# Half-precision row transposes by transposing DMAs in a cross-attention and expert kernel

## The chip, the cores and the metric

One core of a Trainium2 chip runs the kernel. The metric is device time in microseconds of one execution. The kernel before takes 740.51 us, the median of 3 runs (737.42 to 745.31).

## What is computed

The reference is one layer on 2048 tokens of width 512: a cross-attention with 32 heads of 16, then a feed-forward part with one shared expert and 16 routed ones, of which each token takes two. Cut to what matters:

```
x = x + xattn(layernorm(x), ctx, pos)          # 32 heads of 16, axial RoPE
h = layernorm(x)                               # the "xn2" of the kernel
shared = (silu(h @ s1.T) * (h @ s3.T)) @ s2.T  # inner width 352
scores = sigmoid(h @ gate_w.T); top 2 of scores + bias, gates = sel / sum(sel)
routed = sum over chosen e of gate * ((silu(h @ w1[e].T) * (h @ w3[e].T)) @ w2[e].T)
x = x + shared + routed
```

## The kernel before

All engines run programs written out by hand, joined by semaphores. Every operand of a large product is split into a high and a low half-precision part, and a product is three matmuls per chunk of 128 (high by high, high by low, low by high). A matmul needs its rows with the model width on the partitions, so each [128 tokens, 2 parts, 512] tile of `xn2` must be transposed in eight 128x128 blocks.

**Attention** is a pipeline over 16 batches of 128 tokens. At its end, ScalarE makes the high part of `xn2` (`xn2_high`) and POOL the low part (`xn2_low`). PE then transposes both (`xn2_transpose`, line 622), ScalarE copies the result from PSUM into `xn2T` (`xn2T_copy`, line 828), and PE multiplies it with the gate weights (`gate_logits`). The first gate and up of the feed-forward part waits for all logits. SP's queue stores `xn2_parts` to HBM as `xn2_dram` and `xn2T` as `xn2T_dram`, and loads `ctx`.

**Shared stage.** The 16 tiles of 128 tokens are sub-tiles n = 0 to 15, two to a pair j. The order on PE is written out: hidden transpose of n (line 699), gate and up of n + 1 (line 692, into `p_qk` and `p_sc`), down of n (line 712). The operand `xeT` of gate and up has two buffers and is loaded from `xn2T_dram`: the first two by SP, the other 14 by ScalarE (`load_rows`, line 944), which issues the load for n + 2 after the gate activation of n + 1. Beside it DVE works out the routing.

**Routed stage.** Tokens are sorted by expert into tiles of 256 slots (two sub-tiles); this input needs 19 tiles, so 38 sub-tiles. POOL gathers the rows of a sub-tile from `xn2_dram` into `xe` (`gather`, line 1472) and scatters the results into the output with addition (`add_rows`, line 1487). PE transposes the gathered rows (`rows_transpose`, line 678) between gate and up and down, and ScalarE copies them from PSUM into `xeT` (`xeT_copy`, line 912). ScalarE and DVE also split the next expert's weights into parts (lines 933 and 940, 1100 and 1096). SP loads an expert's weights (1408 KB for gate and up, 704 KB for down) only where the tile's expert is a new one.

## Time and profile before

| | |
|---|---|
| median of 3 runs | 740.51 us |
| profiled execution | 740.43 us, span 738.7 us |
| mean granted clock of PE | 0.976 |
| busy: PE, DVE, ACT, POOL | 92%, 71%, 54%, 50% of the span |
| attention | 0 to 373 us |
| shared stage | 373 to 476 us |
| routed stage | 476 us to the end |

The busy shares are of the profiled execution's span. PE, TensorE's matmuls, is busy nearly all the time in each stage, except in the first 45 us and at the end of attention (340 to 373 us), where it waits for other engines. A wait is read from the brackets behind a row of the timeline: how long the engine was idle before it, and what released it.

### The profile page before, as it was taken

Reading aid. Unit: us, or ns where it says so; the run is one execution under the profiler, and the core shown is the slowest. Engines: PE = TensorE matmul, PEld = TensorE weight load, DVE = VectorE, ACT = ScalarE, POOL = GpSimd, SP = SyncE. Lnnn points to the kernel's source line nnn. Section 1 sums busy time; section 2 is a strip of 40 time slices with the busy share of each in tenths; the row PEclk is TensorE's granted clock in tenths of the full one; section 3 lists DMA queues with packets and bytes.
Section 4 is the critical chain, followed back from the end, with each engine's and each line's share of the span. In section 5 each row is a group of like instructions: output and inputs, shape, how many; then the busy total and the mean of one; then the engine's idle time right before and its main releaser. Section 6 shows DMA issues by size and latency. Waiting matters only on the chain.

```text
span 738.7 us, 20567 instructions
## 1 busy us (share of the span) xinstructions
PE 681.3 (92%) x7616; PEld 436.3 (59%) x7616; DVE 525.3 (71%) x992; ACT 397.6 (54%) x666; POOL 366.1 (50%) x439
## 2 busy tenths in 40 slices
PE   3389999999999999998489998999999999999992
PEld 1156666666666666666245665666666666666661
DVE  5968888888888888876537772467676666767671
ACT  4255666665666666665521111366666656666661
POOL 5455556655556665542100001145776557777662
PEclk9789999999999999999979999999999999999997
DMA  9610111000011110000113256258568875555952
GB/s 300 222 48 9 37 38 39 34 21 35 21 35 35 35 35 28 28 29 31 59 57 100 72 182 225 73 145 250 97 192 239 254 199 94 98 94 78 278 121 31
DMA packets 37601, 73.88 MB, mean 100 GB/s; under 512 B 3920, under 2 KB 8048, under 8 KB 37552
## 3 DMA queue, kind: packets, MB, share of 16 engines
q1 hardware_dynamic: 26736, 48.81, 19.2%
q0 software_dynamic: 8800, 20.73, 14.9%
q10 hardware_dynamic: 2016, 3.67, 1.7%
q8 instruction: 33, 0.54, 0.3%
q14 instruction: 16, 0.13, 0.1%
HBM read 69.85 MB, written 22.81 MB: 125 GB/s over the span
## 4 chain that ended last, share of the span: by engine, by line
PE 83%; DVE 6%; DMA 4%; issue 3%; POOL 2%; ACT 1%; POOLq 0%; SPq 0%; DVEq 0%; ACTq 0%
PE p_sc L712 13%; PE p_qk L692 13%; PE p_sc L692 12%; PE p_v L486 8%; PE p_qk L486 7%; PE p_pv L586 5%; PE p_st L534 4%; PE p_pv L589 4%; PE p_sc L566 3%; PE p_sc L549 3%; PE p_pv L596 2%; PE p_tr L678 2%; PE p_v L699 2%; PE p_sc L569 2%; DMA xeT<-xn2T_dram 2%
## 5 line engine op out<-in xcount | busy, mean ns | idle before, releaser
L809 ACT ACTIVATE prob<-p_sc 128x512 f32<-128x512 f32 x128 | 71.4, 601 | 58.8 <-PE p_sc L569 58.8
L1073 DVE TENSOR_REDUCE negmax<-p_sc 128x4 f16<-128x512 f32 x128 | 82.7, 685 | 8.6 <-PE p_sc L549 8.0
L924 ACT CAST hiddenT<-p_v 128x384 f16<-128x384 f32 x54 | 25.9, 479 | 108.7 <-PE p_v L699 108.7
L712 PE MATMUL p_sc<-used_twice,hiddenT 128*128 128x512 f16 (+1 forms) x342 | 80.1, 379 | 0.0
L1192 DVE TENSOR_TENSOR hidden<-p_sc,act_g 128x352 f32<-128x352 f32 x55 | 28.8, 524 | 68.5 <-PE p_sc L692 47.0
L1467 POOL COPY from_at<-from_rows 128x1 uint32 (+1 forms) x40 | 33.0, 825 | 89.0 <-DVE from_rows L1309 85.8
L692 PE MATMUL p_sc<-used_twice,xeT 128*128 128x352 f16 x468 | 76.2, 313 | 0.0
L692 PE MATMUL p_qk<-used_twice,xeT 128*128 128x352 f16 x468 | 76.2, 312 | 0.0
L1487 POOL DMA_INDIRECT out<-prob,to_at x38 | 67.8, 1786 | 11.0 <-issue 10.1
L1100 DVE SCALAR_TENSOR_TENSOR used_twice<-w,used_twice 128x704 f16<-128x704 f32 x80 | 67.7, 887 | 2.5
L692 PEld LDWEIGHTS p_sc<-used_twice,xeT 128*128 128x128 f16 x468 | 45.8, 98 | 24.0
L486 PE MATMUL p_qk<-used_twice,xnT 128*128 128x512 f16 x192 | 51.7, 396 | 8.5 <-issue 8.5
L912 ACT COPY xeT<-p_tr 128x1024 f16<-128x1024 f16 x40 | 40.5, 1013 | 34.2 <-PE p_tr L678 33.8
L933 ACT ACTIVATE used_twice<-w 128x704 f16<-128x704 f32 x80 | 58.6, 783 | 0.0
L692 PEld LDWEIGHTS p_qk<-used_twice,xeT 128*128 128x128 f16 x468 | 45.7, 98 | 20.5
L1446 POOL TENSOR_TENSOR xn_parts<-xn,xn_parts 128x512 f16<-128x512 f32 x16 | 18.5, 1156 | 70.8 <-ACT xn_parts L836 70.8
L586 PE MATMUL p_pv<-prob,used_twice_too 128*32 128x128 f32 x1024 | 52.6, 277 | 0.5 <-DVE attn L1092 0.5
L1209 DVE TENSOR_SCALAR prob<-p_sc,gate_at 128x512 f32<-128x512 f32 x38 | 28.5, 751 | 33.4 <-PE p_sc L712 30.8
L589 PE MATMUL p_pv<-prob,sum_row 128*32 128x128 f32 x1024 | 51.5, 273 | 0.0
L712 PEld LDWEIGHTS p_sc<-used_twice,hiddenT 128*128 128x128 f16 (+1 forms) x342 | 31.8, 98 | 31.5
L486 PE MATMUL p_v<-used_twice,attnT 128*128 128x512 f16 x192 | 47.6, 380 | 2.0 <-POOL attnT L1442 2.0
L1472 POOL DMA_INDIRECT xe<-xn_dram,from_at x40 | 45.4, 1135 | 8.1 <-issue 3.6
(186 smaller groups left out, 1551.3 us busy)
## 6 DMA issues: line engine op xcount, KB each, us to landing
w<-e SPq DMA_DIRECT2D x20, 1408.0 KB
w<-e SPq DMA_DIRECT2D x20, 512.0 KB
out<-stream SPq DMA_DIRECT2D x17, 256.0 KB, 2.1
xn_dram<-xn_parts SPq DMA_DIRECT2D x16, 256.0 KB, 2.0
xn2T_dram<-xn2T SPq DMA_DIRECT2D x16, 256.0 KB, 2.0
w<-e SPq DMA_DIRECT2D x20, 192.0 KB
stream<-x SPq DMA_DIRECT2D x1, 3584.0 KB, 16.8
xeT<-xn2T_dram ACTq DMA_DIRECT2D x14, 256.0 KB, 2.7
```

What stands on the lines that cost most here:

```text
L486: mm = pe.matmul(to, rows[:, r_part, c, :], w[:, w_part, c, :], start=(c == 0 and r_part + w_part == 0), stop=(c == last and r_part == 1))
L586: pe.matmul(p_pv[2 * HD * n:2 * HD * (n + 1), block], vpad[:, par, head(c, n), :], prob[:, c % RING, n * P:(n + 1) * P], start=(c % 4 == 0 ...
L589: mm = pe.matmul(pv_sum[2 * HD * n:2 * HD * (n + 1), :], sum_row[:, c % 4, :], prob[:, c % RING, n * P:(n + 1) * P], start=False, stop=(c ...
L692: mm = pe.matmul(p_out, xeT[:, u, x_part, c, :], w[:, w_part, c, at:at + INNER], start=(c == 0 and x_part + w_part == 0), stop=(c == KC - ...
L712: mm = pe.matmul(p_y[u][:], hiddenT[0:k, h_part, c, :], w[0:k, w_part, c, :], start=(c == 0 and h_part + w_part == 0), stop=(c == len(ICH) ...
L809: act.activation(prob[:, c % RING, :], p_scored(c)[:], ACT.Exp, scale=SCALE).then_inc(exp_ready, 1)
L912: act.copy(xeT[:, u], p_xT).then_inc(sems.xeT_ready, 1)
L933: act.activation(split[par][0][:, 0, c], w13[:, par, c], ACT.Copy, scale=W_SCALE).then_inc(hi13, 1)
L1073: dve.tensor_reduce(negmax[:, c % 2, at:at + CH], p_scored(c)[:].rearrange("p (h t) -> p h t", t=P), AX_X, ALU.max, negate=True).then_inc( ...
L1100: dve.scalar_tensor_tensor(to[0][:, 1, c], w13[:, par, c], W_SCALE, to[0][:, 0, c], ALU.mult, ALU.subtract).then_inc(lo13, 1)
L1472: pool.indirect_dma_start(out=xe[:, u].rearrange("p a d -> p (a d)"), out_offset=None, in_=xn2_dram, in_offset=bass.IndirectOffsetOnAxis(a ...
L1487: pool.indirect_dma_start(out=out, out_offset=bass.IndirectOffsetOnAxis(ap=to_at[:, par, u:u + 1], axis=0), in_=ye[:, par, u], in_offset=N ...
```

## The change

In attention SP's queue transposes `xn2_parts` from SBUF straight into `xn2T` behind the store of the same rows; PE's transposes and ScalarE's copy are gone, and so is `xn2T_dram`. In the shared stage the loads of `xeT` become transposing DMAs from `xn2_dram`. In the routed stage ScalarE issues a transposing DMA from `xe` into `xeT`, in the place of its copy, once the gather has landed and the buffer is free (`rows_turn`); a copy of one column into `carrier_act` stands ahead of it and carries the waits. POOL's next gather into `xe` waits for that DMA to land where it waited for PE. ScalarE issues its first transposing DMA after those of SP have landed.

```diff
--- before.py
+++ after.py
@@ -65,8 +65,6 @@
     def __init__(self, sem):
         self.xT_loaded = [sem(f"xT_loaded{n}") for n in range(2)]
         self.xe_gathered = [sem(f"xe_gathered{n}") for n in range(2)]
-        self.xeT_done = sem("xeT_done")
-        self.xeT_ready = sem("xeT_ready")
         self.g_done = sem("g_done")
         self.u_done = sem("u_done")
         self.act_ready = sem("act_ready")
@@ -91,7 +89,6 @@
 
 
         xn2_dram = nc.dram_tensor("xn2_dram", [T, 2 * DIM], F16, kind="Internal").ap()
-        xn2T_dram = nc.dram_tensor("xn2T_dram", [T, 2 * DIM], F16, kind="Internal").ap()
 
 
         stream = sb("stream", [P, B, DIM])
@@ -113,7 +110,7 @@
         ones16 = sb("ones16", [P, P], F16)
 
 
-        carrier_dve, carrier_pool = sb("carrier_dve", [P, 1]), sb("carrier_pool", [P, 2 * SUB + 1])
+        carrier_dve, carrier_act, carrier_pool = sb("carrier_dve", [P, 1]), sb("carrier_act", [P, SUB + 1]), sb("carrier_pool", [P, 2 * SUB + 1])
         minus_half = sb("minus_half", [P, 1])
         angle = sb("angle", [P, B, ROT])
         turns = sb("turns", [P, B, ROT])
@@ -257,9 +254,9 @@
 
         attnT_hi = sem("attnT_hi"); attnT_lo = sem("attnT_lo"); gate_parts = sem("gate_parts")
         wo_done = sem("wo_done"); ln2_step = sem("ln2_step"); rstd2_ready = sem("rstd2_ready")
-        xn2T_done = sem("xn2T_done"); xn2T_ready = sem("xn2T_ready")
+        xn2T_ready = sem("xn2T_ready")
         xn2_hi = sem("xn2_hi"); xn2_lo = sem("xn2_lo")
-        xn2_stored = sem("xn2_stored"); xn2T_stored = sem("xn2T_stored"); gate_done = sem("gate_done"); logits_kept = sem("logits_kept")
+        xn2_stored = sem("xn2_stored"); gate_done = sem("gate_done"); logits_kept = sem("logits_kept")
 
         gate_exp = sem("gate_exp"); route = sem("route"); masks_ready = sem("masks_ready")
         counted = sem("counted"); experts_known = sem("experts_known"); slots_known = sem("slots_known")
@@ -398,11 +395,8 @@
                 sp.wait_ge(xn2_stored, b * 16 + 16)
                 sp.dma_start(xn2_dram[bass.ds(b * P, P)], xn2_parts[:, par].rearrange("p a d -> p (a d)")).then_inc(xn2_stored, 16)
 
-            def store_xn2T(b, par):
-                sp.wait_ge(xn2T_ready, b + 1)
-                if later(b, 1):
-                    sp.wait_ge(xn2T_stored, b * 16)
-                sp.dma_start(xn2T_dram[bass.ds(b * P, P)], xn2T[:].rearrange("p a c t -> p (a c t)")).then_inc(xn2T_stored, 16)
+            def turn_xn2(b, par):
+                sp.dma_start_transpose(xn2T[:].rearrange("p a c t -> p (a c) t"), xn2_parts[:, par].rearrange("p a d -> p (a d)")).then_inc(xn2T_ready, 16)
 
             def load_ctx(b, half):
                 if later(b, 2):
@@ -413,11 +407,11 @@
             def step(b, on):
                 on(4, load_ctx)
                 on(-1, store_xn2)
-                on(-1, store_xn2T)
+                on(-1, turn_xn2)
                 if isinstance(b, int) and b == B - 1:
-                    sp.wait_ge(xn2T_stored, 2 * 16)
+                    sp.wait_ge(xn2_stored, 3 * 16)
                     for n in range(2):
-                        sp.dma_start(xeT[:, n].rearrange("p a c t -> p (a c t)"), xn2T_dram[n * P:(n + 1) * P]).then_inc(sems.xT_loaded[n], 16)
+                        sp.dma_start_transpose(xeT[:, n].rearrange("p a c t -> p (a c) t"), xn2_dram[n * P:(n + 1) * P]).then_inc(sems.xT_loaded[n], 16)
 
             load_ctx(2, 0)
             load_ctx(3, 1)
@@ -610,20 +604,13 @@
                 if c == KC - 1:
                     mm.then_inc(wo_done, 1)
 
-            def xn2_transpose(b, par):
-                pe.wait_ge(xn2_lo, b + 1)
+            def gate_logits(b, par):
+                pe.wait_ge(xn2T_ready, b * 16 + 16)
 
                 last_xn = B if isinstance(b, int) and b + 4 > B else b + 4
                 pe.wait_ge(xnT_lo, last_xn)
                 if later(b, 1):
                     pe.wait_ge(logits_kept, b)
-                for a in range(2):
-                    for c in range(KC):
-                        mm = pe.transpose(p_xT[:, a, c, :], xn2_parts[:, par, a, c * P:(c + 1) * P], ident16[:])
-                mm.then_inc(xn2T_done, 1)
-
-            def gate_logits(b, par):
-                pe.wait_ge(xn2T_ready, b + 1)
                 if not later(b, 1):
                     pe.wait_ge(gate_parts, 2)
                 for c in range(KC):
@@ -637,7 +624,6 @@
                 on(-3, spread_recip, 1)
                 on(-1, project_q, 0)
                 on(-2, scores, 2)
-                on(-4, xn2_transpose)
                 on(-1, project_q, 1)
                 on(-2, scores, 3)
                 on(-1, project_q, 2)
@@ -671,19 +657,10 @@
             pipeline(step, pe, 0, B + 3, 6, (B - 6) // 2, ahead=[xn_transpose])
 
 
-            def rows_transpose(n, u, j):
-                pe.wait_ge(sems.xe_gathered[u], (j - (SHARED - 1)) * 16)
-                for a in range(2):
-                    for c in range(KC):
-                        mm = pe.transpose(p_xT[:, a, c, :], xe[:, u, a, c * P:(c + 1) * P], ident16[:])
-                mm.then_inc(sems.xeT_done, 1)
-
             def gate_up(n, u, j, par, kind):
 
-                if kind == "shared":
-                    pe.wait_ge(sems.xT_loaded[u], j * 16 + 16)
-                else:
-                    pe.wait_ge(sems.xeT_ready, n - (B - 1))
+                pe.wait_ge(sems.xT_loaded[u], j * 16 + 16)
+                if kind == "routed":
                     pe.wait_ge(lo13, split_no(j) * KC)
                 w = split["shared" if kind == "shared" else par][0]
                 for p_out, at, done in ((p_g, 0, sems.g_done), (p_u, INNER, sems.u_done)):
@@ -743,8 +720,6 @@
                         gate_up(n + 1, 1, j, par, kinds[0])
                     elif kinds[1]:
                         gate_up(n + 1, 0, j + 1, 1 - par, kinds[1])
-                    if kinds[1] == "routed":
-                        rows_transpose(n + 2, u, j + 1)
                     down(n, u, j, par, kinds[0])
                     if kinds[0] == "shared":
                         if n == COUNTED:
@@ -820,19 +795,12 @@
                     act.wait_ge(wo_done, b)
                 act.copy(attnT[:, 0], attn_rows).then_inc(attnT_hi, 1)
 
-            def xn2T_copy(b, par):
-                act.wait_ge(xn2T_done, b + 1)
-                if later(b, 1):
-                    act.wait_ge(gate_done, b)
-                    act.wait_ge(xn2T_stored, b * 16)
-                act.copy(xn2T[:], p_xT).then_inc(xn2T_ready, 1)
-
             def xn2_high(b, par):
                 act.wait_ge(ln2_step, b * 5 + 5)
                 if later(b, 1):
                     act.wait_ge(xn2_stored, b * 16)
                 if later(b, 2):
-                    act.wait_ge(xn2T_done, b - 1)
+                    act.wait_ge(xn2T_ready, b * 16 - 16)
                 act.copy(xn2_parts[:, par, 0], xn2[:, par]).then_inc(xn2_hi, 1)
 
             def ctx_high(b, par):
@@ -870,7 +838,6 @@
             act.wait_ge(zeroed, 1)
 
             def step(b, on):
-                on(-5, xn2T_copy)
                 on(0, ctx_high)
                 on(-2, v_copy)
                 on(-3, exp, 0)
@@ -906,10 +873,11 @@
             act.wait_ge(logits_kept, B)
             act.activation(score[:], logits[:], ACT.Exp, scale=-1.0).then_inc(gate_exp, 1)
 
-            def xeT_copy(n, u):
-                act.wait_ge(sems.xeT_done, n - (B - 1))
+            def rows_turn(n, u, j):
+                act.wait_ge(sems.xe_gathered[u], (j - (SHARED - 1)) * 16)
                 act.wait_ge(sems.u_done, n - 1)
-                act.copy(xeT[:, u], p_xT).then_inc(sems.xeT_ready, 1)
+                act.copy(carrier_act[:, u:u + 1], minus_half[:])
+                act.dma_start_transpose(xeT[:, u].rearrange("p a c t -> p (a c) t"), xe[:, u].rearrange("p a d -> p (a d)")).then_inc(sems.xT_loaded[u], 16)
 
             def gate_act(n):
                 act.wait_ge(sems.g_done, n + 1)
@@ -941,9 +909,11 @@
 
             def load_rows(n, u):
                 act.wait_ge(sems.u_done, n - 1)
-                act.dma_start(xeT[:, u].rearrange("p a c t -> p (a c t)"), xn2T_dram[n * P:(n + 1) * P]).then_inc(sems.xT_loaded[u], 16)
-
-            act.wait_ge(xn2T_stored, B * 16)
+                act.dma_start_transpose(xeT[:, u].rearrange("p a c t -> p (a c) t"), xn2_dram[n * P:(n + 1) * P]).then_inc(sems.xT_loaded[u], 16)
+
+            act.wait_ge(xn2_stored, B * 16 + 16)
+            for n in range(2):
+                act.wait_ge(sems.xT_loaded[n], 16)
             gate_act(0)
 
             def pair(j, par, kinds):
@@ -960,7 +930,7 @@
                 if kinds[1] == "shared":
                     load_rows(n + 2, 0)
                 elif kinds[1]:
-                    xeT_copy(n + 2, 0)
+                    rows_turn(n + 2, 0, j + 1)
                 hT_high(n + 1)
                 if split_next:
                     w2_high(j + 1, 1 - par, 0)
@@ -972,9 +942,15 @@
                 if kinds[1] == "shared":
                     load_rows(n + 3, 1)
                 elif kinds[1]:
-                    xeT_copy(n + 3, 1)
-
-            pairs(pair, act)
+                    rows_turn(n + 3, 1, j + 1)
+                else:
+                    for u in range(SUB):
+                        act.nop().then_inc(sems.xT_loaded[u], 16)
+
+            used = pairs(pair, act)
+            for u in range(SUB):
+                act.wait_ge(sems.xT_loaded[u], used * 16 + (SHARED + 1) * 16)
+            act.copy(carrier_act[:, SUB:SUB + 1], minus_half[:])
 
 
         @block.vector
@@ -1467,7 +1443,7 @@
                 pool.tensor_copy(from_at[:, par, u:u + 1], from_rows[:, bass.ds(q, 1)]).then_inc(from_copied, 1)
                 pool.wait_ge(from_copied, q + 1)
                 if later(j, SHARED + 1):
-                    pool.wait_ge(sems.xeT_done, (j - SHARED) * SUB + (u - 1))
+                    pool.wait_ge(sems.xT_loaded[u], j * 16)
                 pool.tensor_tensor(carrier_pool[:, u:u + 1], minus_half[:], minus_half[:], ALU.mult)
                 pool.indirect_dma_start(out=xe[:, u].rearrange("p a d -> p (a d)"), out_offset=None, in_=xn2_dram,
                                         in_offset=bass.IndirectOffsetOnAxis(ap=from_at[:, par, u:u + 1], axis=0)).then_inc(sems.xe_gathered[u], 16)
```

PE, the loop of the routed stage, before (rows of one sub-tile and a half; `p_tr` is the PSUM tile of the transposed rows, `xe` the gathered rows, `xeT` the transposed ones):

```order
L699 MATMUL p_v<-ident,hidden 128x128 [waits hidden_ready]
L699 MATMUL p_v<-ident,hidden 128x128 x2
L692 MATMUL p_qk<-used_twice,xeT 128x352 [waits lo13,xeT_ready]
L692 MATMUL p_qk<-used_twice,xeT 128x352 x11
L692 MATMUL p_sc<-used_twice,xeT 128x352 x12
L678 MATMUL p_tr<-ident,xe 128x128 [waits xe_gathered0]
L678 MATMUL p_tr<-ident,xe 128x128 x7
L712 MATMUL p_sc<-used_twice,hiddenT 128x512 [waits y_ready,lo2,hT_lo,hT_hi]
L712 MATMUL p_sc<-used_twice,hiddenT 128x512 x8
```

The same of the changed kernel:

```order
L676 MATMUL p_v<-ident,hidden 128x128 [waits hidden_ready]
L676 MATMUL p_v<-ident,hidden 128x128 x2
L669 MATMUL p_qk<-used_twice,xeT 128x352 [waits lo13,xT_loaded1]
L669 MATMUL p_qk<-used_twice,xeT 128x352 x11
L669 MATMUL p_sc<-used_twice,xeT 128x352 x12
L689 MATMUL p_sc<-used_twice,hiddenT 128x512 [waits y_ready,lo2,hT_lo,hT_hi]
L689 MATMUL p_sc<-used_twice,hiddenT 128x512 x8
```

The eight transposes between gate and up and down are gone, and gate and up waits for a DMA's semaphore (`xT_loaded`) where it waited for ScalarE's copy (`xeT_ready`).

ScalarE, the same loop, before (`act_g` is the gate activation, `used_twice` the split weights):

```order
L918 ACTIVATE act_g<-p_qk 128x352 [waits hidden_ready,g_done]
L933 ACTIVATE used_twice<-w 128x704 x2
L910 REGISTER_ALU
L912 COPY xeT<-p_tr 128x1024 [waits u_done,xeT_done]
L924 CAST hiddenT<-p_v 128x384 [waits y_done,hT_done]
```

The same of the changed kernel:

```order
L886 ACTIVATE act_g<-p_qk 128x352 [waits hidden_ready,g_done]
L901 ACTIVATE used_twice<-w 128x704 x2
L877 ISA
L879 COPY carrier_act<-minus_half 128x1 [waits u_done,xe_gathered0]
L880 DMA_TRANSPOSE xeT<-xe 128x8x128
L892 CAST hiddenT<-p_v 128x384 [waits y_done,hT_done]
```

The copy of 1024 columns has become one small copy with the waits and one DMA issue, at the same place in ScalarE's program.

SP's queue, one batch of attention's loop, before (`ctx_sb` is the context of a later batch):

```order
L411 DMA ctx_sb<-ctxT 128x2x128
L397 REGISTER_ALU
L398 ISA [waits xn2_lo]
L399 ISA [waits xn2_stored]
L399 DMA xn_dram<-xn_parts 128x1024
L405 DMA xn2T_dram<-xn2T 128x1024 [waits xn2T_stored,xn2T_ready]
```

The same of the changed kernel:

```order
L405 DMA ctx_sb<-ctxT 128x2x128
L394 REGISTER_ALU
L395 ISA [waits xn2_lo]
L396 ISA [waits xn2_stored]
L396 DMA xn_dram<-xn_parts 128x1024
L399 DMA_TRANSPOSE xn2T<-xn_parts 128x8x128
```

The store of the transposed rows is replaced by the transposing DMA, which has no wait of its own.

## Rows read from the trace of the kernel before

**Rows 1.** the page: PE's busy time, and the chain that ended last

```profile
PE 681.3 (92%) x7616; PEld 436.3 (59%) x7616; DVE 525.3 (71%) x992; ACT 397.6 (54%) x666; POOL 366.1 (50%) x439
...
PE 83%; DVE 6%; DMA 4%; issue 3%; POOL 2%; ACT 1%; POOLq 0%; SPq 0%; DVEq 0%; ACTq 0%
```

**Rows 2.** timeline of a routed pair, PE: start, us, engine, line, operation

```profile
700.11 1.95 PE L692 MATMUL p_qk<-used_twice,xeT 128*128 128x352 f16 x12
...
703.69 0.61 PE L678 MATMUL p_tr<-ident,xe 128*128 128x128 f16 x8
704.13 2.11 PE L712 MATMUL p_sc<-used_twice,hiddenT 128*128 128x512 f16 x9
...
706.41 1.95 PE L692 MATMUL p_qk<-used_twice,xeT 128*128 128x352 f16 x12
```

**Rows 3.** timeline of the same pair, ACT

```profile
702.10 0.47 ACT L918 ACTIVATE act_g<-p_qk 128x352 f32<-128x352 f32 x1
702.46 1.46 ACT L933 ACTIVATE used_twice<-w 128x704 f16<-128x704 f32 x2
...
708.76 0.62 ACT L940 ACTIVATE used_twice<-w 96x512 f16<-96x512 f32 x1
```

**Rows 4.** timeline of a shared tile; ACTq: DMA issue on ScalarE

```profile
414.49 1.95 PE L692 MATMUL p_qk<-used_twice_too,xeT 128*128 128x352 f16 x12
...
416.48 0.47 ACT L918 ACTIVATE act_g<-p_qk 128x352 f32<-128x352 f32 x1 [1.31 <-PE p_qk L692]
416.49 0.33 ACTq L944 DMA_DIRECT2D xeT<-xn2T_dram  x1
...
420.35 1.95 PE L692 MATMUL p_qk<-used_twice_too,xeT 128*128 128x352 f16 x12
```

**Rows 5.** DMA issues of the run: count, size, median us to landing

```profile
xn_dram<-xn_parts SPq DMA_DIRECT2D x16, 256.0 KB, 2.0
...
xeT<-xn2T_dram ACTq DMA_DIRECT2D x14, 256.0 KB, 2.7
...
xe<-xn_dram,from_at POOLq DMA_INDIRECT x40, 4.2
...
out<-prob,to_at POOLq DMA_INDIRECT x38
```

**Rows 6.** DMA queue q1 in 202.9:206, 207.7:209.5, 25:27: packets, MB, share of engines

```profile
q1 hardware_dynamic: 144, 0.26, 22.5%
...
q1 hardware_dynamic: 271, 0.13, 25.8%
...
q1 hardware_dynamic: 272, 0.06, 15.0%
```

**Rows 7.** timeline, shared stage: a load issued beside weight loads, and PE after it

```profile
439.90 0.33 ACTq L944 DMA_DIRECT2D xeT<-xn2T_dram  x1
...
445.35 1.96 PE L692 MATMUL p_qk<-used_twice_too,xeT 128*128 128x352 f16 x12 [1.43 <-DMA xeT<-xn2T_dram]
```

**Rows 8.** timeline of SP's queue: a weight load done, and one skipped

```profile
504.01 0.38 SPq L443 DMA_DIRECT2D w<-e  x1
...
605.48 0.09 SPq L443 DMA_DIRECT2D w<-e  x1
```

**Rows 9.** timeline of one steady batch of attention, POOL and PE

```profile
201.48 1.16 POOL L1446 TENSOR_TENSOR xn_parts<-xn,xn_parts 128x512 f16<-128x512 f32 x1 [4.05 <-ACT xn_parts L836]
...
203.98 0.62 PE L622 MATMUL p_tr<-ident,xn_parts 128*128 128x128 f16 x8
...
215.20 0.45 PE L486 MATMUL p_tr<-gate,xn2T 128*128 128x16 f16 x12
```

**Rows 10.** timeline of attention's end

```profile
369.24 1.15 POOL L1446 TENSOR_TENSOR xn_parts<-xn,xn_parts 128x512 f16<-128x512 f32 x1 [1.38 <-ACT xn_parts L836]
...
372.59 0.49 PE L486 MATMUL p_tr<-gate,xn2T 128*128 128x16 f16 x12 [1.10 <-ACT xn2T L828]
```

**Rows 11.** windows: stretch, length, busy PE, PEld, DVE, ACT, POOL, PEclk, DMA, GB/s

```profile
350.00:356.00 6.00, 4.73 (x132) 3.83 (x128) 1.83 (x3) 2.68 (x7) 0.49 (x1) 1.00 0.01 3
```


## The prediction

> **What bounds the kernel now.** I read the page first: PE is busy 92% of the span and the chain that ended last runs through PE for 83% [rows 1]. So work taken off PE counts, and work taken off ScalarE or POOL counts only through what it delays. Then the timelines, stage by stage, to see who delivers to PE and with how much to spare.
>
> In the routed stage PE runs without a gap: gate and up for the next sub-tile, eight transposes, down, the hidden transpose, gate and up again. From one gate-and-up to the next it is 706.41 - 700.11 = 6.30 us, and the eight transposes hold PE from 703.69 to 704.13, 0.44 us [rows 2]. In the shared stage there are none, and the period is 420.35 - 414.49 = 5.86 us [rows 4]. 5.86 + 0.44 = 6.30, so each sub-tile pays exactly for its transposes.
>
> **Removed from PE.** 40 groups of eight on the gathered rows (the gathers are x40 [rows 5]), 0.44 us each; 38 of them lie in full routed sub-tiles (the scatter is x38). In attention 16 groups, at the same price; in the drain PE waits anyway, so I count 13: 5.8 us. On ScalarE 56 copies out of PSUM go as well, but it is no bound, so nothing is counted. The most the change can save is 38 x 0.44 + 5.8 = 22.5 us.
>
> **What takes their place, and when it must be done.** The operand of gate and up now comes by a transposing DMA. In the shared stage ScalarE already issues a plain load at that place. It goes out at 416.49, with the start of the gate activation, not after its end: 2.00 us after gate and up began [rows 4]. PE wants the tile at 5.86. With about 0.1 us for the two semaphores, the period of a sub-tile is the larger of 5.86 and 2.1 + L, L being the time from issue to landing. **The threshold is L = 3.76 us.**
>
> In the routed stage the new issue stands behind one or two more activations. Its sequencer need only have passed their waits; as in [rows 4] I let it run ahead of them, so 2.0 us there too: the gate activation starts at 702.10, 1.99 after 700.11 [rows 2, 3]. If it does not run ahead, it goes out when the queued activations are done: after 702.46 + 1.46 = 703.92, so 4.0 us with the small copy (even sub-tiles), or after 709.38, 3.2 us (odd ones) [rows 3]. That is a rival.
>
> **L.** No row shows a transposing DMA. Of the same 256 KB tile, the store lands in 2.0 us, the plain load in 2.7, the gather by POOL in 4.2 [rows 5]. A plain load is 128 packets of 2 KB. From the queue's share times the window times 16 engines, over the packets, one takes 0.225 x 3.1 x 16 / 144 = 77 ns; 512-byte packets take 0.258 x 1.8 x 16 / 271 = 27 ns, and a mix of 220 bytes on average 0.150 x 2 x 16 / 272 = 18 ns [rows 6]. So small packets cost more per byte. Plain: 8 per engine x 77 = 0.62 us of the 2.7. In 256-byte runs (one column of 128 values) 64 x 18 = 1.15 us: L = 3.2. In 64-byte runs 256 x 18 = 4.5 us: L = 6.6. The lower end is the plain 2.7, or 2.0 if nothing is read from HBM; the upper 6.6. I take 4.5, in the middle and beside the gather's 4.2, the only row in which this tile is rearranged on its way.
>
> The Trainium skill (Advanced Engine Details and Errata, X-Bar Transpose (TRN2)) says that transposing DMAs on this chip are as fast as regular ones. By that L would be 2.7 and the sum that of the first rival; no row here shows it.
>
> **Beside weight loads** L grows. A plain load issued at 439.90 among weight loads let PE start only at 445.35, so it took about 5.35, 2.65 more than 2.7 [rows 7]. In the routed stage the real weight loads are those of 0.34 to 0.41 us on SP's queue, the skipped ones 0.07 to 0.11 [rows 8]; 9 gate/up loads between 491 and 694 us are real. Each is issued shortly before the turn of one of the pair's two sub-tiles and has 1.4 MB to move. So 9 turns get L + 2.65.
>
> **The sum at L = 4.5**, against the profiled run of 740.4 us (span 738.7; the median of the runs is 740.5, so nothing is to be shifted):
> - routed, clear: 29 x (6.6 - 6.30) = +8.7
> - routed, beside weight loads: 9 x (9.25 - 6.30) = +26.6
> - shared: 12 x (6.6 - 5.86) = +8.9; the two already late go from 2.7 to 4.5, +3.6
> - attention: -5.8
> - attention's end: rows done at 370.39, gate at 372.59 [rows 10], 2.2 us with PE transposes and a ScalarE copy; now the store's issue, then L, 4.9: +2.7
> - sum +44.7, so **785 us**.
>
> Edits put at nothing. The 16 turns in attention from SP's queue, behind the store: rows ready at 202.64, gate wants them at 215.20 [rows 9], and L is far below 12 us. The store of the transposed rows to HBM goes, off the path. ScalarE's added small copies: it is 54% busy [rows 1]. A sequencer held by the transposing DMA: ScalarE's next work for PE, the hidden copy, comes 5.86 us after gate and up began and the issue 2.00 [rows 4], so up to 3.9 us of hold is covered. The gather now waits for the turn to land rather than for PE, some 2.5 us later; it then needs about 2 us for its issue and 4.2 to land, and the turn that wants it comes a pair (13.2 us) after the last: 2 us are left, and POOL's queue behind it (the scatter) has them too. PE's clock: it was 1.00 with PE busy 4.73 of 6 us [rows 11]; at L = 4.5 it is busy 89% in clear sub-tiles. If stalls grew past that and the clock halved, gate and up would take twice 3.58 us [rows 2].
>
> **Rivals.**
> 1. *The turn is hidden (L up to 3.76) but weight loads still delay 9 of them.* At 2.7: 29 x -0.44 + 9 x (7.45 - 6.30) - 5.8 + 0.9 = -7.3, 733; at 3.7: 745. For: plain load 2.7. Against: small packets [rows 6].
> 2. *Faster: hidden, and the collisions too.* It decides if the turn's packets are served between those of the weight load instead of behind it; then L stays under 3.76 everywhere: -16.7 - 5.8 + 0.9 = -21.6, 719. For: turn and load come by different queues. Against [rows 7].
> 3. *Longer yet: ScalarE issues late, or L is 5.5 to 6.6.* Late at 4.5: even sub-tiles 8.6, odd 7.8, so 19 x 2.3 + 19 x 1.5 + 9 x 2.65, with 12.5 shared, -5.8 and +2.7: +105, 846. L = 6.6 issued early: 29 x 2.4 + 9 x 5.05 + 12 x 2.84 + 7.8 - 5.8 + 4.8 = +156, 896.
> 4. *The blocks go one after another.* A tile is eight 128x128 blocks; if each pays the 1.4 us by which even the store's landing exceeds its packets (2.0 - 0.62), L is 8 x 1.4 + 0.6 = 11.8 and the period 13.9: 38 x 7.6 + 14 x 8.0 - 5.8 + 10 = +405, 1145. The order of instructions shows one DMA per tile, which speaks against it.
>
> For rival 4 the Trainium skill (VectorE: DVE Perf Modes, The three transpose paths) gives 1309 ns for a 128x128 block by DMA against 390 by TensorE; eight in series make 10.5 us, an estimate that would put the time near 1075. It speaks against this change, and no row here bears it out.
>
> That it does not do what it says I put at nothing: the built order has the DMAs in place of the matmuls.
>
> **Chances.** Forecast (L 3.8 to 5.5, 745 to 838) 0.38; rival 1 0.22; rival 2 0.17; rival 3 0.15; rival 4 0.08. The forecast's own range is 745 to 840. The range with room for the others is 720 to 870: it drops rival 4, half of rival 3 and the edge of rival 2. About 1% (7.4 us) is what a measurement here can tell from no change. Faster by more than that: rival 2 and the edge of rival 1, 0.20. Within: most of rival 1 and the lowest edge of the forecast, 0.20. Slower: 0.60.
>
> **What would show it.** DMA_TRANSPOSE issues on ScalarE's queue with a landing near 4.5 us, and 2.0 us after gate and up began; PE idle before gate and up, released by that DMA, 0.7 us in most sub-tiles and about 3 beside real weight loads; the routed period above 6.30; no idle time at the gate matmuls in attention. Wrong if PE's wait there is absent (rival 1 or 2), if the issue stands 3 to 4 us after gate and up (rival 3), or if the gate in attention waits (rival 4). It would be wrong in a way I did not see if POOL's gathers came too late for the turns.

## The result: 790.7 us against 739.1, slower by 6.6%

The changed kernel takes 790.71 us, the median of 4 runs (784.61 to 792.61); the kernel before takes 739.13 (737.42 to 745.31). The ratio is 1.0661, with a 95% interval of 1.0612 to 1.071. Ratios here and below are worked out over the single runs, without those of a slower state in which some runs of a kernel fall (over 1.5% above its fastest run), so they differ a little from the quotient of two medians, which is 1.070 here. The profiled execution took 784.61 us with a span of 782.7, so it is the fastest of the four and 6 us shorter than the median. The forecast of 785 was met within its range; how it was met is another matter.

### The page after

Busy time, queue q10 (ScalarE's DMAs: packets, MB, share of 16 engines), the chain that ended last, by engine, and the group of gate and up with its idle time. They answer to [rows 1].

```profile
PE 679.5 (87%) x7168; PEld 415.3 (53%) x7168; DVE 526.9 (67%) x992; ACT 345.3 (44%) x651; POOL 366.3 (47%) x439
...
q10 hardware_dynamic: 57024, 14.16, 11.9%
...
PE 69%; DMA 15%; DVE 9%; issue 4%; ACT 1%; POOL 1%; SPq 0%; POOLq 0%; DVEq 0%; ACTq 0%
...
L669 PE MATMUL p_qk<-used_twice,xeT 128*128 128x352 f16 x468 | 86.0, 339 | 41.8 <-DMA xeT<-xe 41.5
```

PE issues 448 matmuls fewer, yet is busy only 1.8 us less. DMA has gone from 4% to 15% of the chain, and 41.5 us of PE's idle time end with the landing of `xeT<-xe`. ScalarE's 54 turning DMAs are made of small pieces: 57024 packets for 14.16 MB, 1056 for each tile of 256 KB and 248 bytes each.

The three kinds of turning DMA, each from the answer on its source line: form, count, issue time in ns (min/median/max), first and last start; then issue to landing in us. Line 880 is the routed stage, 912 the shared stage, 399 attention. They answer to [rows 5].

```profile
L880 ACTq DMA_TRANSPOSE xeT<-xe x40: 1247/1257/1731, 478.2 to 765.2; - x40
...
DMA to landing us min/median/max: 3.1/3.4/13.6
```

```profile
L912 ACTq DMA_TRANSPOSE xeT<-xn_dram x14: 1247/1249/1433, 382.2 to 472.3; - x14
...
DMA to landing us min/median/max: 3.0/3.3/7.9
```

```profile
L399 SPq DMA_TRANSPOSE xn2T<-xn_parts x16: 1277/1297/1384, 82.0 to 369.2; - x16
...
DMA to landing us min/median/max: 3.1/3.1/4.5
```

The median, 3.1 to 3.4 us, is under the threshold of 3.76. The maximum of line 880 is four times the median: the experiments below show that nearly all of the loss is in that tail.

### A turn in the clear

The timeline of the changed kernel, 654 to 668 us (start, duration, engine, line, operation; ACTq is ScalarE's DMA issue), and the DMA queues in 664:666 (packets, MB, share of 16 engines):

```profile
654.69 1.95 PE L669 MATMUL p_qk<-used_twice,xeT 128*128 128x352 f16 x12
...
660.71 1.96 PE L669 MATMUL p_qk<-used_twice,xeT 128*128 128x352 f16 x12
...
662.79 1.30 ACTq L880 DMA_TRANSPOSE xeT<-xe  x1
...
666.58 1.66 PE L669 MATMUL p_qk<-used_twice,xeT 128*128 128x352 f16 x10
```

```profile
q10 hardware_dynamic: 1051, 0.26, 66.7%
```

The DMA is issued 2.08 us after gate and up began. Nearly all of its packets move within two microseconds: 0.667 x 2 x 16 / 1051 = 20 ns each. Gate and up has no bracket: PE waits for nothing. The periods alternate between 6.02 and 5.87, 5.94 on average, 0.36 less than the 6.30 of [rows 2].

### A turn beside a real weight load

The same loop at 610 to 628 us, the worst of the nine real loads; SPq is SyncE's issue of weights (437 the 1408 KB for gate and up, 439 the first of the two parts for down):

```profile
610.95 1.96 PE L669 MATMUL p_qk<-used_twice,xeT 128*128 128x352 f16 x12
...
611.18 0.38 SPq L437 DMA_DIRECT2D w<-e  x1
...
613.03 1.37 ACTq L880 DMA_TRANSPOSE xeT<-xe  x1
...
616.17 0.37 SPq L439 DMA_DIRECT2D w<-e  x1
...
626.77 1.64 PE L669 MATMUL p_qk<-used_twice,xeT 128*128 128x352 f16 x5 [9.79 <-DMA xeT<-xe]
```

The DMA queues of the same kernel in 613:617, 617:619, 619:621 and 621:623 (q1 is SyncE's queue with the weights, q0 POOL's gathers and scatters):

```profile
q1 hardware_dynamic: 365, 1.03, 75.7%
q0 software_dynamic: 58, 0.22, 16.5%
```

```profile
q10 hardware_dynamic: 419, 0.11, 56.2%
q1 hardware_dynamic: 138, 0.35, 52.3%
```

```profile
q10 hardware_dynamic: 213, 0.05, 118.4%
...
q1 hardware_dynamic: 9, 0.01, 2.1%
```

```profile
q10 hardware_dynamic: 310, 0.08, 98.7%
...
q1 hardware_dynamic: 34, 0.07, 9.2%
```

Two things happen one after the other. From 613 to 617 not one packet of q10 is recorded: the turn, issued 1.85 us behind the load, stands until most of the load has moved. From 617 on its packets move, but a packet takes 43 ns (0.562 x 2 x 16 / 419) while the last of the load moves, then, with hardly any packet of the load left, 178 and 102, against 20 in the clear. (A share of 118.4% of the engines' time means that the records of packets overlap, so these are times in flight.) The tile lands 13.6 us after its issue, and PE has waited 9.79.

Not every load costs that much. Another one, and the queues in 587:589:

```profile
580.41 0.38 SPq L437 DMA_DIRECT2D w<-e  x1
...
583.36 1.32 ACTq L880 DMA_TRANSPOSE xeT<-xe  x1
...
589.16 3.54 PE L669 MATMUL p_qk<-used_twice,xeT 128*128 128x352 f16 x12 [1.86 <-DMA xeT<-xe]
```

```profile
q10 hardware_dynamic: 774, 0.19, 74.9%
```

Here the turn is issued 2.95 us behind the load, a packet takes 31 ns (0.749 x 2 x 16 / 774), and PE waits 1.86 us. The nine real loads fall into two groups. Five (issued at 494.37, 514.33, 558.54, 611.18 and 720.36) go out 1.85 to 1.93 us ahead of a turn; the next gate and up waits 5.17, 5.62, 8.36, 9.79 and 2.66 us, 31.6 of the 41.5. The other four (580.41, 597.10, 634.75 and 736.75) go out 2.77 to 3.78 us ahead of a turn, and the next gate and up waits 0.25 to 1.86 us. No run changed this distance alone.

### Where the 44 us went

The routed stage between the same two gate-and-ups (38 periods), by windows: length, busy time of PE, PEld, DVE, ACT and POOL with counts, granted clock, DMA share, GB/s. First the changed kernel, then the kernel before:

```profile
482.27:763.09 280.82, 239.14 (x1368) 139.07 (x1369) 164.29 (x248) 119.78 (x247) 159.66 (x221) 0.93 0.83 176
```

```profile
478.79:719.01 240.22, 239.73 (x1676) 153.04 (x1673) 165.07 (x247) 154.69 (x247) 159.02 (x221) 1.00 0.68 164
```

The stage is 40.6 us longer. PE's idle time in it is 41.7 us, where it was 0.5: +41.2. The transposes' 38 x 0.44 = 16.7 us are gone, so PE should be busy 223.0 us; it is busy 239.1, 16.1 more: **the granted clock** is 0.93 instead of 1.00. After most of the longer waits gate and up runs at the lower of the two clock levels (1.2 instead of 2.4 GHz) for a while; an example:

```profile
525.83 3.70 PE L669 MATMUL p_qk<-used_twice,xeT 128*128 128x352 f16 x12 [5.62 <-DMA xeT<-xe]
```

3.70 us instead of 1.95, and the granted clock of 525.80 to 529.53 is 0.50. Six gate-and-ups are so, with 3.25 to 3.70 us, behind waits of 1.86 to 9.79 us; one behind a wait of 1.93 us keeps its 1.96. Without the waits in them, the six periods are 12.5 us longer than six of 5.94.

So 41.2 - 16.7 + 16.1 = 40.6. (About 3 of the 16.1 are clear periods of 5.94 where 6.30 - 0.44 would be 5.86.)

The shared stage is 3.7 us longer (373.11 to 482.27, where it was 373.35 to 478.79), by one wait: that for the turn issued at 439.49, behind the first weight loads (from 434.61 on).

```profile
447.42 1.94 PE L669 MATMUL p_qk<-used_twice_too,xeT 128*128 128x352 f16 x6 [3.91 <-DMA xeT<-xn_dram]
```

Attention came out even. Its end, which answers to [rows 10]:

```profile
368.77 0.34 SPq L396 DMA_DIRECT2D xn_dram<-xn_parts  x1
369.15 1.30 SPq L399 DMA_TRANSPOSE xn2T<-xn_parts  x1
...
372.34 0.49 PE L480 MATMUL p_tr<-gate,xn2T 128*128 128x16 f16 x12 [8.32 <-DMA xn2T<-xn_parts]
```

The rows are done at about 368.7, 1.6 us before 370.39; then the gate takes 3.6 us to begin where it took 2.2. It starts 0.25 us earlier than before.

### The profile page after: what moved, and what is told of

Read it like the earlier page. It is cut to its first block, busy times and chain, and to the rows that moved or that the text cites. A ratio compares the mean times of both kernels' runs of the same rounds, so it can differ in the third digit from the quotient of the medians.

```text
span 782.7 us, 19616 instructions
## 1 busy us (share of the span) xinstructions
PE 679.5 (87%) x7168; PEld 415.3 (53%) x7168; DVE 526.9 (67%) x992; ACT 345.3 (44%) x651; POOL 366.3 (47%) x439
## 3 DMA queue, kind: packets, MB, share of 16 engines
q10 hardware_dynamic: 57024, 14.16, 11.9%
## 4 chain that ended last, share of the span: by engine, by line
PE 69%; DMA 15%; DVE 9%; issue 4%; ACT 1%; POOL 1%; SPq 0%; POOLq 0%; DVEq 0%; ACTq 0%
PE p_qk L669 15%; DMA xeT<-xe 12%; PE p_sc L689 10%; PE p_sc L669 10%; PE p_v L480 7%; PE p_pv L580 4%; PE p_st L528 4%; DVE negmax L1049 4%; PE p_pv L583 4%; PE p_qk L480 3%; PE p_sc L560 3%; PE p_pv L590 2%; PE p_sc L563 2%; PE p_v L676 2%; PE p_sc L543 2%
## 5 line engine op out<-in xcount | busy, mean ns | idle before, releaser
L669 PE MATMUL p_qk<-used_twice,xeT 128*128 128x352 f16 x468 | 86.0, 339 | 41.8 <-DMA xeT<-xe 41.5
L1443 POOL COPY from_at<-from_rows 128x1 uint32 (+1 forms) x40 | 38.7, 968 | 93.1 <-DVE from_rows L1285 92.2
L669 PE MATMUL p_sc<-used_twice,xeT 128*128 128x352 f16 x468 | 78.7, 319 | 0.0
L1463 POOL DMA_INDIRECT out<-prob,to_at x38 | 65.0, 1712 | 12.3 <-issue 12.0
L886 ACT ACTIVATE act_g<-p_qk 128x352 f32<-128x352 f32 x55 | 25.6, 465 | 85.4 <-PE p_qk L669 85.3
L1447 POOL TENSOR_TENSOR carrier_pool<-minus_half 128x1 f32<-128x1 f32 x40 | 13.2, 329 | 102.7 <-DMA xeT<-xe 102.6
L480 PE MATMUL p_qk<-used_twice,xnT 128*128 128x512 f16 x192 | 51.6, 395 | 8.7 <-issue 8.7
L480 PE MATMUL p_v<-used_twice,attnT 128*128 128x512 f16 x192 | 51.3, 403 | 2.5 <-POOL attnT L1418 2.4
L689 PEld LDWEIGHTS p_sc<-used_twice,hiddenT 128*128 128x128 f16 (+1 forms) x342 | 33.4, 98 | 35.4
L1448 POOL DMA_INDIRECT xe<-xn_dram,from_at x40 | 42.5, 1064 | 11.6 <-issue 8.2
## 6 DMA issues: line engine op xcount, KB each, us to landing
stream<-x SPq DMA_DIRECT2D x1, 3584.0 KB, 16.7
```

Of the source, the lines that this page charges most:

```text
L480: mm = pe.matmul(to, rows[:, r_part, c, :], w[:, w_part, c, :], start=(c == 0 and r_part + w_part == 0), stop=(c == last and r_part == 1))
L669: mm = pe.matmul(p_out, xeT[:, u, x_part, c, :], w[:, w_part, c, at:at + INNER], start=(c == 0 and x_part + w_part == 0), stop=(c == KC - ...
L689: mm = pe.matmul(p_y[u][:], hiddenT[0:k, h_part, c, :], w[0:k, w_part, c, :], start=(c == 0 and h_part + w_part == 0), stop=(c == len(ICH) ...
L1443: pool.tensor_copy(from_at[:, par, u:u + 1], from_rows[:, bass.ds(q, 1)]).then_inc(from_copied, 1)
L1448: pool.indirect_dma_start(out=xe[:, u].rearrange("p a d -> p (a d)"), out_offset=None, in_=xn2_dram, in_offset=bass.IndirectOffsetOnAxis(a ...
L1463: pool.indirect_dma_start(out=out, out_offset=bass.IndirectOffsetOnAxis(ap=to_at[:, par, u:u + 1], axis=0), in_=ye[:, par, u], in_offset=N ...
```

## The experiments

The expectations name the theories by letters. Theory C: a turning DMA is cheap, and the loss is its collisions with the real weight loads. Its rivals: D, the turn's way costs by itself (through ScalarE's queue or later gathers); K, it is the clock alone; X, it is the transposing: a transposing DMA beside a load is slowed far beyond its share. Theory B came later: backlog, a turn waits for what is queued and moving when it is issued. It asks which load, and whether the order of issue decides. Where a kernel was run with one execution, its time stands alone, beside the median of the kernel before on that chip.

**Where it is: the routed stage out, the loads out.** e3 keeps the changes in attention and in the shared stage and gives PE's transposes and ScalarE's copy back to the routed stage:

```diff
+                if kinds[1] == "routed":
+                    rows_transpose(n + 2, u, j + 1)
...
-                    rows_turn(n + 2, 0, j + 1)
+                    xeT_copy(n + 2, 0)
```

> The changed kernel with the routed stage of the kernel before (PE transposes the gathered rows, ScalarE copies them): attention and shared stage alone are changed. By the two traces attention's end comes 0.2 us earlier and the shared stage takes 3.7 us longer (two turns beside the first weight loads). Theory C and every theory that puts the loss in the routed stage: 740 to 745 us, the same as before. A rival by which attention or the shared stage carries a part of the 50 us through the clock or a later start of POOL: 755 or more.

Measured: 746.97 us, ratio 1.0026 [0.9984, 1.0068]. That is just above the 740 to 745 expected and no clear difference: the loss is in the routed stage.

e4 (the changed kernel) and e5 (the kernel before) mark no tile as one with a new expert, which leaves out the real weight loads of the routed stage after its first two tiles:

```diff
-                dve.tensor_tensor(tile_new[:, 2:TILES], tile_expert[:, 2:TILES], tile_expert[:, 0:TILES - 2],
+                dve.tensor_tensor(tile_new[:, 2:TILES], tile_expert[:, 2:TILES], tile_expert[:, 2:TILES],
```

> The changed kernel without the weight loads of the routed stage after the first two tiles: the condition of each load is always false, and the routed tiles compute with the weights of the first two experts. 9 gate/up loads and their down loads are left out. Theory C: all waits for turns in the routed stage go and its period is 5.94 us throughout: 726 to 732 us (the shared stage keeps its 4 us). If gathers and scatters, which stay, slow the turns: above 745. Rival D: above 755.

> The kernel before without the weight loads of the routed stage after the first two tiles (the same are left out as in the changed kernel's run without them; the routed tiles compute with the weights of the first two experts). If weight loads cost only where a transposing DMA stands beside them, nothing moves here: 737 to 745 us. A rival by which the loads slow gathers or scatters and so PE in any kernel: below 732.

Measured: 730.28 us for the changed kernel, 736.57 for the one before (medians of the full kernel before: 742.02 and 741.37). Without loads the changed kernel is 6.3 us below the other. These are single runs, and the full kernel before alone spreads from 738.1 to 746.8, so that small gap is not shown by the times; the shorter period in the clear (5.94 against 6.30) supports it. The large one is plain: the loads cost the changed kernel 60 us and the kernel before 5. Its turns on line 880:

```profile
L880 ACTq DMA_TRANSPOSE xeT<-xe x40: 1247/1249/1302, 477.1 to 710.8; - x40
...
  PE p_qk L669: 1.4, 3
...
DMA to landing us min/median/max: 3.1/3.2/4.6
```

PE waits 1.4 us in all for 40 turns, and the clock granted from 476 to 710 is 1.00. Theory C stands, and D with its 755 or more falls: no loads, no tail, no clock loss.

**Is it the transposing?** e6 replaces the transposing DMA of the routed stage by a plain copy with runs of 2 KB; e7 by a plain copy in runs of 256 bytes (the destination's rows are padded so that they can't be joined). Neither turns the rows, so both leave the transposition out.

```diff
-                act.dma_start_transpose(xeT[:, u].rearrange("p a c t -> p (a c) t"), xe[:, u].rearrange("p a d -> p (a d)")).then_inc(sems.xT_loaded[u], 16)
+                act.dma_start(xeT[:, u].rearrange("p a c t -> p (a c t)"), xe[:, u].rearrange("p a d -> p (a d)")).then_inc(sems.xT_loaded[u], 16)
```

```diff
-        xeT = sb("xeT", [P, 2, 2, KC, P], F16)
+        xeT = sb("xeT", [P, 2, 2, KC, P + 16], F16)[:, :, :, :, 0:P]
...
+                act.dma_start(xeT[:, u].rearrange("p a c t -> p (a c) t"), xe[:, u].rearrange("p a (c t) -> p (a c) t", c=KC)).then_inc(sems.xT_loaded[u], 16)
```

> The changed kernel with plain DMAs in place of the 40 transposing ones from xe to xeT, from the same place in ScalarE's queue, of the same 256 KB, 128 packets of 2 KB; the rows are copied untransposed. Theory X (a transposing DMA beside a load is slowed far beyond its share): a plain one beside a load takes no more than the 5.4 us that one took in the kernel before, so at most 1.6 us of wait at each of 9 to 12, no fall of the clock: 730 to 748 us. Rival (any DMA at that place waits as long, because the load's packets are served first): 770 or more.

> As the run with plain 2 KB packets, but both sides in runs of 256 bytes: 1024 packets as the transposing DMA has. It tells the number of small packets from the transposing itself. If it is the transposing: 730 to 750 us, as with 2 KB packets or a little more. If each small packet waits for one large packet of the load (64 per engine x 112 ns = 7 us): long waits as with the transposing DMA, 765 us or more.

Measured: 764.27 and 783.47 us (before: 741.37). Line 880 of e6, then of e7:

```profile
L880 ACTq DMA_DIRECT2D xeT<-xe x40: 472/472/537, 476.4 to 744.6; - x40
...
DMA to landing us min/median/max: 2.3/2.5/8.0
```

```profile
L880 ACTq DMA_DIRECT2D xeT<-xe x40: 601/602/712, 475.1 to 763.7; - x40
...
DMA to landing us min/median/max: 2.9/3.1/11.2
```

Theory X falls: with a plain copy in pieces of the same size PE waits 42.7 us for the copies, where it waited 41.5 for the turns, the time is within 1.1 us of the changed kernel's fastest run, and the median landing is near (3.1 against 3.4). The expectation for e6 was missed: large pieces halve the loss (23 us of 42, with 19.6 us of waits) but do not remove it. Around a load issued at 611.86 and a copy issued at 613.71, e6's queues in 618:619 and 619:620 read (q10 has none before):

```profile
q1 hardware_dynamic: 97, 0.27, 75.5%
q10 hardware_dynamic: 16, 0.03, 8.4%
```

```profile
q10 hardware_dynamic: 91, 0.18, 45.9%
q1 hardware_dynamic: 66, 0.17, 44.0%
```

The plain copy's first packets too appear only 4.3 us or more after its issue, behind most of the load; then its 128 large packets are nearly all through in 3 us, where the small ones took 8 to 9 in the changed kernel (617 to 626). So the tail has two parts: standing behind the load, whatever is copied, and the number of packets after it.

The Trainium skill (DMA: Bandwidth & Descriptors, Queues, rings and completion order) says that each DMA engine takes the queues for which it has work in turn and switches only between packets, by which it means groups of about 9 to 17 descriptors (each moves one piece), at most 64. A packet of the profile is such a piece: the gate/up load's are of 2816 bytes (1.03 MB in 365), so 1408 KB are 512 of them, 32 for each engine if they are spread evenly. With the page's typical group a turn would start among the load's pieces, and the trace disagrees, with no q10 packet recorded in 613:617 of the changed kernel; with one group of 32 it would stand behind the whole load. How the load was grouped no run here shows.

**Which load?** e9 cuts the routed stage's gate/up load to 16 columns of one chunk, e10 the down loads to 16 columns (64-byte pieces); both leave most of those weights stale.

```diff
+                part = slice(0, 16) if kept else slice(0, W13)
+                sp.dma_start(w13[:, par, 0:1 if kept else KC, part], e13[bass.ds(e, 1)].rearrange("o (c p) n -> p (o c) n", p=P)[:, 0:1 if kept else KC, part], **new).then_inc(w13_loaded[par], 16)
```

```diff
+                part = slice(0, 16) if kept else slice(0, DIM)
+                sp.dma_start(w2[:, par, 0:2, part], e2[bass.ds(e, 1), 0:2 * P].rearrange("o (c p) n -> p (o c) n", p=P)[:, :, part], **new).then_inc(w2_loaded[par], 16)
```

> The changed kernel with the routed stage's gate/up loads (after the first two tiles) cut from 1408 KB to 8 KB each, the down loads (704 KB) whole; the routed tiles compute with the first two experts' gate/up weights but for that piece. Theory B (backlog: a turn waits for the bytes that are queued and moving when it is issued, the more so for its 1024 small packets): the gate/up load is the one issued 1.9 us ahead of a turn, so nearly all waits go, and 728 to 738 us are left. Rival (the down load does it, since the turn's packets were seen moving beside it): 755 or more.

> The changed kernel with the down loads of the routed stage cut from 704 KB to some 12 KB, the gate/up loads whole. Theory B: the turn still stands behind 1408 KB, so it lands after some 7 to 8 us instead of up to 13.6; waits of 2 to 4 us at 9 turns: 745 to 765 us. Rival (the down load does it): below 738. Rival (each load matters alone as much as both): 775 or more.

Measured: 738.88 and 789.34 us (before: 739.90). From issue to landing (min/median/max) the turns take 3.1/3.5/5.3 us in e9 and 3.1/3.5/11.6 in e10.

With the 704 KB of the down loads alone the turns land within 5.3 us and the loss against the kernel before is gone; with the 1408 KB alone it is all there (43.5 us of waits). I had expected the two to share it. The down loads are not free either: in e9 PE still waits 8.7 us, at ten turns, and the run is 8.6 us above e4, single runs both, so they take about what the change would gain. e10 keeps the down loads' pieces, at 64 bytes each, so it shows that beside the large load the down load's bytes don't matter, not that an empty queue would be the same.

**Does the order of issue decide?** e1 holds the gate/up load until the up half of gate and up is done, some 2 us behind a turn's issue, and the down load until the turn has landed; e2 holds only the gate/up load.

```diff
+                gate_ups = (j - 2) * SUB + 1 if kept else (j - SHARED + FIRST) * SUB + 2
+                sp.wait_ge(sems.u_done, gate_ups)
...
+                sp.wait_ge(*((sems.xT_loaded[0], j * 16) if kept else (sems.u_done, gate_ups + 1)))
```

> The changed kernel, but SP issues the gate/up weights of a later expert only when gate and up of the tile's first sub-tile is done on PE, and the down weights only when the next turn has landed, so that no weight load moves data while a transposing DMA does. Theory C (collisions): the routed stage lost 41.5 us of PE waits and some 14 us of halved clock to turns issued beside real weight loads, and nothing to the other turns, whose period is 5.94 us against 6.30 before. Then the waits go: 782.7 - 41.5 - 14 - about 4 in the shared stage, span 720 to 728, 722 to 730 us, faster than the kernel before by 1.5 to 2.5%. Rival D (the turn's way costs by itself, through ScalarE's held sequencer, POOL's later gathers, or loads that now come too late): stays above 755 us. Rival K (the clock alone): the waits stay, only their size changes, 765 or more.

> As the paced kernel, but only the gate/up weights (1408 KB) wait for PE; the down weights (704 KB) follow them on SP's queue as before and so move data when the next turn does. Theory C says that what counts is any real load beside a turn: waits stay at about 9 turns, smaller, since 704 KB are left of 2112: 735 to 765 us. A rival by which only the large load that begins just ahead of a turn matters: as the fully paced kernel, 722 to 730 us. Rival D: 755 or more, as the paced one.

Measured: e1 759.62 us, ratio 1.0208 [1.0162, 1.0253]; e2 788.34, 1.06 [1.0545, 1.0655]. Both expectations were missed, and both times fit the number of rival D (755 or more), which e4 had ruled out as the cause of the loss. K's case (765 or more, the waits staying) did not come in e1. Line 883 of e1:

```profile
  PE p_qk L672: 28.1, 19
...
DMA to landing us min/median/max: 3.1/4.0/7.2
```

Pacing both loads takes the tail from 13.6 to 7.2 us and gives 31 us back, but now 19 turns wait a little, 28.1 us in all. Held alone, the gate/up load is followed by the down load 1.1 us later and meets the next turn (47.1 us of waits in e2). A load of this size does not fit between two turns 5.9 us apart: in the kernel before, the packets of the one issued at 567.01 are seen from 568 to past 574.

e12 issues the turn earlier, ahead of the gate activation; e8 does that and paces both loads.

```diff
-                gate_act(n + 1)
...
                     rows_turn(n + 2, 0, j + 1)
+                gate_act(n + 1)
```

> The changed kernel with each turn issued just ahead of the gate activation, 0.2 us after gate and up began instead of 2.1, so that it has 5.6 us instead of 3.8; weight loads as in the changed kernel, now issued at the same moment as the turn. Theory B: a turn issued with the load, not 1.9 us behind it, shares the engines with it from the start and lands after 6 to 8 us: waits of 1 to 3 us, 745 to 765 us, faster than the changed kernel. Rival (the load is served first however the turn lies): as the changed kernel, 780 or more.

> The paced kernel with two further moves: ScalarE issues each turn just ahead of the gate activation, so about 0.3 us after gate and up began instead of 2.1, and SP issues the gate/up weights when the gate half is done, 1.8 us after. A turn has 5.5 us then instead of 3.8, and its packets are meant to lie before those of the load. Theory C with amplification by overlap (the paced run still had 28 us of waits, at turns whose packets met the load's tail): waits under 8 us, 722 to 734 us, faster than the kernel before. If turns are slowed by the load however they lie: as the paced run, 750 to 762. If ScalarE, held by the issue ahead of its gate activation, or gathers that now come too late bound the stage: above 745, with waits of ScalarE for the gather.

Measured: e12 791.96 us, 1.0594 [1.053, 1.0657]; e8 772.63, 1.0302 [1.0215, 1.0389]. Both expectations were missed; e12 came by its rival's number (780 or more) and e8 by its last one (above 745, with waits of ScalarE for the gather). e12's timeline at a load:

```profile
595.55 0.37 SPq L437 DMA_DIRECT2D w<-e  x1
595.62 1.25 ACTq L880 DMA_TRANSPOSE xeT<-xe  x1
...
606.04 2.24 PE L669 MATMUL p_qk<-used_twice,xeT 128*128 128x352 f16 x7 [4.69 <-DMA xeT<-xe]
```

and its queues in 599:600 (q10 has none before):

```profile
q1 hardware_dynamic: 133, 0.37, 103.0%
q10 hardware_dynamic: 20, 0.01, 2.2%
```

A turn issued 0.07 us after the load has no packet recorded before 599, 3.4 us on. Issuing it two microseconds sooner gains nothing while the load goes out first. In e8 the load does come later, but ScalarE waits 15.9 us for gathers, at 12 turns, which it does not in e1 or in the changed kernel, and the turns land with a median of 5.2 us, where e1 has 4.0. How much of e8's loss is late gathers and how much the loads was not told apart.

**A mixture.** e11 turns the first sub-tile of each pair by DMA and the second by PE, with one turn in 12 us to pay for.

```diff
-                    rows_turn(n + 3, 1, j + 1)
+                    xeT_copy(n + 3, 1, j + 1)
```

> A mixture: in the routed stage the tile's first sub-tile is turned by the DMA and the second, whose turn would be issued 1.9 us after the gate/up load, is transposed by PE and copied by ScalarE as in the kernel before; attention and shared stage as changed. Theory B: the turn that is left is issued some 8 us after the gate/up load and 3 after the down load, nearly clear; 19 periods gain 0.4 us each, some 4 us are lost in the shared stage and a few at real loads: 730 to 742 us, the same as the kernel before or a little faster. Rival (any turn in a pair with a real load waits long): 750 or more.

Measured: 748.44 us, 1.0113 [1.008, 1.0147]: slower than the kernel before by 1.1% and outside the 730 to 742 expected. With 20 turns PE still waits for 11 of them:

```profile
PE p_qk L681 <- DMA xeT<-xe: 13.0, 11, 2.8
```

Half the transposes' time is worth 19 x 0.44 = 8.4 us, and the waits cost 13.0. No version that computes everything beat the kernel before.

## Why the prediction came out right, and which of its steps did not

- **The threshold and the issue.** Right: the issue stands 2.08 us after gate and up began (2.0 put), and ScalarE runs ahead in even and odd sub-tiles. Rival 3's late issue did not come, nor rival 4's blocks in series: eight blocks land together in 3.1 us. The Trainium skill (VectorE: DVE Perf Modes, The three transpose paths) has 1309 ns for a block by DMA; as a price to be paid eight times it does not hold in this kernel.
- **L in the clear: 4.5 put, 3.1 to 3.4 measured.** This is the first mis-sized term. The right value was the prediction's own bound in 256-byte runs (3.2), which it had worked out and passed over for a value in the middle. So the 29 clear sub-tiles, +8.7 put, gained 0.36 each, and the 12 clear turns of the shared stage cost nothing. The Trainium skill (Advanced Engine Details and Errata, X-Bar Transpose (TRN2)) calls a transposing DMA as fast as a regular one; the runs agree where the pieces are equal (3.4 against 3.1) and less so against 2 KB pieces (2.5).
- **L beside weight loads: 7.15 put, up to 13.6 measured.** The second, and the larger. The prediction took the delay of a plain load of 2 KB packets [rows 7] as an addition of 2.65 us to any DMA. It is no constant: it is the rest of the load, plus the turn's packets, at 31 to 178 ns each in place of 20 in the windows above. In waits of PE the 9 sub-tiles were to cost 9 x (9.25 - 5.86) = 30.5 us; 41.5 came, spread over 14 gate-and-ups.
- **The clock: put at nothing,** with the remark that it would cost if the stalls grew. They did, and it cost about 13 us of the 16.1.
- **Shared and attention.** +12.5 put, +3.7 measured: one turn met the first loads, the others were hidden. Attention -5.8 and +2.7 put; the rows are ready only 1.6 us earlier, the end costs 1.4 more, and the gate starts 0.25 us earlier. That 13 x 0.44 us did not arrive was not followed up by a run of its own; e3, with both parts, shows no difference.

By stages: routed +35.3 put and +40.6 measured, shared +12.5 and +3.7, attention with its end -3.1 and -0.25. So +44.7 was put and +44.2 came in the profiled run (784.6 against 740.4), by errors that cancel: too much for clear turns, attention's end and the shared stage, too little for the collisions and the clock. That it came so near is luck, and the profiled run is the fastest of its kernel: by the medians of the result +51.6 came. What was right is the direction and one mechanism, a turn that meets a weight load. Rival 1 ("hidden, but weight loads still delay some") describes this trace better than the forecast does; its price per collision was wrong by a factor of three: 4.6 us of waits for each of the 9 loads on average, where it put 7.45 - 5.86 = 1.59.

**What stays open.** The runs show that the turn stands behind the load and then has slow packets, that both need the large load, and that it is not the transposing. Why small packets stay slow for some 5 us after the load has gone in the worst collision (67 to 155 packets a microsecond in 619:623, by the four one-microsecond windows), and hardly in the one of 580.41, is not shown; the scatter with addition and the gather run at that time, and no run took them out. That the order comes from how descriptors are made rather than from the DMA engines was not tried either. The clock's share was read from windows and periods and not isolated by a run.

## What to carry to other kernels

When work moves from a compute engine to a DMA that must land within one short period, price the worst landing and not the median: look for the largest transfer that shares the DMA engines, and take the time until it is through, plus the small transfer's packets, as the least for the landing of the one issued behind it. A copy of 256 KB as 1024 pieces is good in the clear and fragile beside a load of 1.4 MB, and if its wait leaves PE idle for several microseconds the clock may have to be paid as well. The quickest test of such a story is to take the big transfers out of both kernels (730 against 737 us here), then to copy the same bytes plainly in pieces of the same size.

## What the runs showed of the hardware that I had not expected

- The issue of a transposing DMA holds ScalarE's queue for 1.25 us (SyncE's for 1.30), that of a plain copy of the same tile 0.47 in 2 KB pieces and 0.60 in 256-byte pieces. No wait of PE was put down to it.
- In three collisions (e12, the changed kernel, e6) a DMA issued on ScalarE's queue 0.07 to 1.9 us after a 1408 KB load on SyncE's had its first packet recorded 3.4 to 4.3 us or more after its issue.
- A 256-byte packet took 20 ns in the clear and 43, 178 and 102 ns in three windows at the end of such a load and after it, 31 ns after another.
